# Delta rule: the fractal mixer's taps move from TensorE to ScalarE and VectorE, TensorE's rounds get a new order and more unread products

## The reference, cut to what matters

```
q, k, v = short_conv(x @ Wq), short_conv(x @ Wk), short_conv(x @ Wv)     # 4 taps along the sequence
...                                       # rotary, l2norm, chunks of 32: T = inverse of a triangular matrix
step:  u_t = ui - wi @ S;  o_i = qi @ S + attn @ u_t;  S_new = g * S + ki^T @ u_t      # 16 chunks, in sequence

def fractal_mixer(x, conv_w):
    out = 2.0 * x
    for i in range(4):
        dil = 2 ** i
        x_shift = jnp.pad(x, ((0, 0), (dil, 0), (0, 0)))[:, :l, :]
        out = out + x_shift * conv_w[i, :, 0] + x * conv_w[i, :, 1]
    return out
frac = rmsnorm(fractal_mixer(x, frac_conv_w), mixer_norm_w)
return core + sigmoid(x @ frac_gate_w + frac_gate_b) * frac
```

## Time and profile before

| what | us |
|---|---|
| median of three runs | 2610.29 (2605.36 to 2612.67) |
| the profiled execution | 2605.69 |
| its span | 2603.9 |
| first state step of round 2 to that of round 3 | 68.0 |
| rounds 3, 4, 5 | 71.0 each |
| rounds 6, 7, 8 | 74.4, 66.1, 56.0 |

### The profile page before, as it was taken

One profiled execution on the slowest core, in us unless ns is written; L12 is line 12 of the kernel. 1 busy time (PEld: TensorE's weight loads), 2 busy tenths in 40 slices (PEclk: granted clock), 3 DMA queues, 4 the chain that ended last, 5 costly groups with the idle time before them and its releaser, 6 DMA issues. The chain is left out here.

```text
span 2603.9 us, 56605 instructions
## 1 busy us (share of the span) xinstructions
PE 2413.8 (93%) x20854; PEld 2007.2 (77%) x20854; DVE 1696.0 (65%) x4060; ACT 1216.3 (47%) x3095; POOL 1334.0 (51%) x1465
## 2 busy tenths in 40 slices
PE   4899999999999999878999999988899999999998
PEld 3788888888888888756777877756677778778776
DVE  4576777767677767576767767326756746747664
ACT  2656666666666666455444445114333333332332
POOL 3676776767676767256555555214522323322322
PEclk8999999999999999989999999988999999999999
DMA  4000100000000000012112111206112112212211
GB/s 141 7 10 9 45 17 11 9 10 10 10 10 9 9 5 5 15 31 45 42 47 49 36 53 43 55 31 187 33 52 68 62 42 74 66 42 62 64 39 58
DMA packets 156688, 105.05 MB, mean 40 GB/s; under 512 B 85168, under 2 KB 134832, under 8 KB 156416
## 3 DMA queue, kind: packets, MB, share of 16 engines
q1 hardware_dynamic: 131072, 62.83, 8.9%
q10 hardware_dynamic: 25344, 38.60, 4.8%
HBM read 80.51 MB, written 20.88 MB: 39 GB/s over the span
## 5 line engine op out<-in xcount | busy, mean ns | idle before, releaser
L920 POOL TENSOR_TENSOR a_bm<-a_bias,a_mask_add 128x512 f32<-128x512 f32 (+3 forms) x512 | 437.8, 871 | 191.0 <-DVE a_nm L674 186.0
L1529 POOL TENSOR_TENSOR m_hid_part<-m_hid,m_hid_part 128x512 fp32r<-128x512 f32 x176 | 239.5, 1361 | 564.1 <-ACT m_hid_part L1438 561.0
L830 ACT ACTIVATE a_S<-a_S,a_nm 128x512 f32<-128x512 f32 (+3 forms) x512 | 289.2, 565 | 346.4 <-DVE a_nm L674 343.6
L674 DVE CUSTOM_DVE_ANT_0 a_S<-a_S,a_bm,a_nsn 128x512 f32<-128x512 f32 (+3 forms) x512 | 275.4, 545 | 141.2 <-PE a_S L438 136.9
L461 PE MATMUL a_O<-a_v,a_PT 128*128 128x64 f32 x2560 | 342.4, 265 | 0.0
L461 PEld LDWEIGHTS a_O<-a_v,a_PT 128*128 128x128 f32 x2560 | 328.4, 193 | 0.0
L1450 ACT ACTIVATE m_hid<-m_G 128x512 f32<-128x512 f32 x176 | 105.4, 599 | 408.4 <-PE m_G L1384 371.3
L438 PE MATMUL a_S<-a_kT,a_qT 128*128 128x384 f32 (+3 forms) x1024 | 284.3, 359 | 3.5 <-DVE a_nm L674 3.0
L1401 PE MATMUL m_Y<-m_hid_part,m_down_high 128*128 128x512 f32 x704 | 257.3, 406 | 11.9 <-POOL m_hid_part L1529 11.1
L1611 DVE TENSOR_TENSOR m_hid<-m_hid,m_U 128x512 f32<-128x512 f32 x176 | 121.0, 687 | 223.6 <-PE m_U L1384 189.7
L1384 PE MATMUL m_G<-m_in,m_gate_high 128*128 128x512 f32 x704 | 251.5, 398 | 1.6 <-POOL m_up_low L1523 1.6
(11 more groups left out here) (314 smaller groups left out, 5240.2 us busy)
## 6 DMA issues: line engine op xcount, KB each, us to landing
m_spread<-s_w ACTq DMA_DIRECT2D x64, 256.0 KB, 3.3
m_spread<-s_w ACTq DMA_DIRECT2D x128, 128.0 KB, 2.9
a_x<-in_x SPq DMA_DIRECT2D x32, 128.0 KB, 2.1
s_hT<-a_hT SPq DMA_DIRECT2D x32, 128.0 KB, 2.1
d_x<-in_x SPq DMA_DIRECT2D x8, 512.0 KB, 4.8
d_h<-s_hT SPq DMA_DIRECT2D x8, 512.0 KB, 5.4
s_xg<-d_xg SPq DMA_DIRECT2D x8, 512.0 KB, 3.1
d_x<-s_xg SPq DMA_DIRECT2D x8, 512.0 KB, 4.5
```

The costliest lines, as they stand in the source:

```text
L674: dve.tensor_tensor_reduce(S[:, n % S_SLOTS, 0:w], SB[n % 2][:, 0:w], bm[:, n % BM_SLOTS, 0:w], -1.0, nsn[:, tile % 2, h:h + 1], ALU.add, ...
L830: act.activation(S[:, n % S_SLOTS, 0:w], S[:, n % S_SLOTS, 0:w], ACT.Exp, scale=-1.0, bias=nm[:, tile % 2, h:h + 1], accum_out=den[:, tile ...
L920: pool.tensor_tensor(bm[:, n % BM_SLOTS, 0:w], bias[:, h, L - w:L], mask_add[b % 2][:, 0:w], ALU.add).then_inc(s["bm_ready"], 1)
L1529: pool.tensor_tensor(hid_part[1][:, q % H_SLOTS], hid[:, q % G_SLOTS], hid_part[0][:, q % H_SLOTS].bitcast(F32), ALU.subtract).then_inc(hi ...
```

## The change

The mixer's sum leaves PE. ACT makes the first tap of each half of the features from the input in SBUF into a new buffer `mx` (`tap`, two pieces for a batch, an activation of 128x512 each). DVE adds the four shifted taps (`mix`, two pieces of four `scalar_tensor_tensor` of 128x512, each behind the one before by a semaphore). PE's `mixer` becomes two transposes of `mx` and moves one round later, to lag F, with `frac`, `fve`, `frs` and `xg` behind it. The diagonal matrices and the ten instructions that made them go. SP's DMAs of `xg` out and of `x` in move one round later too, and its load of the next input waits for `mix_ready`, `proj_psum` and `gates_psum` in place of `mixer_psum`.

PE's table gets a new order: `proj` 4 goes from segment 0 to the end of segment 1, `au` 1 from segment 2 to segment 1, `core` 0 comes before `TZ`, `uw` before `qkT` in segments 8 to 10. Five `warm` pieces are added in segments 1, 4, 6, 8 and 10, of one unread product each, in every round that has a batch in the recurrence. `fast` becomes three products for batch 6 and stays one for batch 7. `warm` takes a bank of the ring as the others do. ACT's table follows.

```diff
-            ("step", 0, R), ("fast", 0, R), ("M", 1, R), ("qp", 0, R), ("proj", 4, IN), ("au", 0, R),
-            ("step", 1, R), ("fast", 1, R), ("M", 2, R), ("mixer", 0, IN), ("M", 3, R),
-            ("step", 2, R), ("fast", 2, R), ("M", 0, R), ("au", 1, R), ("z", 0, IN),
-            ("step", 3, R), ("fast", 3, R), ("proj", 5, IN), ("z", 1, IN), ("au", 2, R),
-            ("step", 4, R), ("fast", 4, R), ("qp", 1, R), ("z", 2, IN), ("Z", 0, F),
-            ("step", 5, R), ("fast", 5, R), ("hold", 0, K), ("hold", 1, K), ("hold", 2, K), ("hold", 3, K), ("onT", 0, K), ("onT", 1, K), ("z", 3, IN), ("mixer", 1, IN),
-            ("step", 6, R), ("fast", 6, R), ("TZ", 0, F), ("core", 0, K), ("au", 3, R),
+            ("step", 0, R), ("fast", 0, R), ("M", 1, R), ("qp", 0, R), ("au", 0, R),
+            ("step", 1, R), ("fast", 1, R), ("M", 2, R), ("warm", 0, R), ("au", 1, R), ("M", 3, R), ("proj", 4, IN),
+            ("step", 2, R), ("fast", 2, R), ("M", 0, R), ("z", 0, IN), ("mixer", 0, F),
+            ("step", 3, R), ("fast", 3, R), ("proj", 5, IN), ("z", 1, IN), ("au", 2, R), ("mixer", 1, F),
+            ("step", 4, R), ("fast", 4, R), ("qp", 1, R), ("Z", 0, F), ("warm", 1, R), ("z", 2, IN),
+            ("step", 5, R), ("fast", 5, R), ("hold", 0, K), ("hold", 1, K), ("hold", 2, K), ("hold", 3, K), ("onT", 0, K), ("onT", 1, K), ("z", 3, IN), ("mixer", 2, F),
+            ("step", 6, R), ("fast", 6, R), ("core", 0, K), ("TZ", 0, F), ("warm", 2, R), ("au", 3, R), ("mixer", 3, F),
             ("step", 7, R), ("fast", 7, R), ("qkT", 0, IN), ("uw", 0, F), ("attn", 0, F),
-            ("step", 8, R), ("fast", 8, R), ("mixer", 2, IN), ("qkT", 1, IN), ("uw", 1, F),
-            ("step", 9, R), ("fast", 9, R), ("core", 1, K), ("qkT", 2, IN), ("uw", 2, F),
-            ("step", 10, R), ("fast", 10, R), ("mixer", 3, IN), ("uw", 3, F), ("qkT", 3, IN),
+            ("step", 8, R), ("fast", 8, R), ("uw", 1, F), ("warm", 3, R), ("qkT", 1, IN),
+            ("step", 9, R), ("fast", 9, R), ("core", 1, K), ("uw", 2, F), ("qkT", 2, IN),
+            ("step", 10, R), ("fast", 10, R), ("uw", 3, F), ("warm", 4, R), ("qkT", 3, IN),
...
-                        unread(fill(name, i, b), B - b)
+                        unread(fill(name, i, b), 1 if b == B - 1 else 3)
...
+                        pe.wait_ge(mix_ready, KD * (b + 1))
                         o = fill(name, i, b)
                         for k in range(KD):
-                            at = PAD + i * P
-                            for j in range(5):
-                                back = 0 if j == 4 else 2 ** j
-                                last = pe.matmul(o[:, k * P:(k + 1) * P],
-                                                 h[b % 2][:, k, at - back:at - back + P], diag[:, k, j],
-                                                 start=j == 0, stop=j == 4)
+                            last = pe.transpose(o[:, k * P:(k + 1) * P], mx[:, k, i * P:(i + 1) * P], ident[:])
...
+                        act.activation(mx[:, i], h[b % 2][:, i, PAD:], ACT.Copy, scale=own[:, i:i + 1]).then_inc(mix_tap, 1)
...
+                        dve.wait_ge(mix_tap, KD * b + i + 1)
+                        for j in range(4):
+                            at = PAD - 2 ** j
+                            ins = dve.scalar_tensor_tensor(out=mx[:, i], in0=h[b % 2][:, i, at:at + L],
+                                                           scalar=frac[:, i, j, 0:1], in1=mx[:, i],
+                                                           op0=ALU.mult, op1=ALU.add)
...
-            ("S", 10, R), ("x1", 1, K),
-            ("S", 11, R), ("fve", 0, IN), ("attn", 1, F), ("low", 0, IN),
-            ("S", 12, R), ("attn", 2, F), ("low", 1, IN), ("attn", 3, F), ("xg", 0, IN),
+            ("S", 10, R), ("x1", 1, K), ("mix", 0, IN),
+            ("S", 11, R), ("fve", 0, F), ("attn", 1, F), ("low", 0, IN), ("mix", 1, IN),
+            ("S", 12, R), ("attn", 2, F), ("low", 1, IN), ("attn", 3, F), ("xg", 0, F),
```

More of the change, by code:

```diff
@@ L1842, in delta_phase @@
         ACT_ROUND = [
[L1843 to L1846, removed]
+            ("ocopy", 0, K), ("ocopy", 1, K), ("M", 1, R), ("silu", 0, IN), ("silu", 1, IN),
+            ("M", 2, R), ("osq", 0, K), ("silu", 2, IN), ("M", 3, R), ("proj", 4, IN),
+            ("M", 0, R), ("silu", 3, IN), ("z", 0, IN), ("frac", 0, F),
+            ("proj", 5, IN), ("z", 1, IN), ("frac", 1, F),
             ("z", 2, IN), ("silu", 4, IN), ("rsq", 0, IN),
-            ("onT", 0, K), ("onT", 1, K), ("z", 3, IN), ("rsq", 1, IN), ("frac", 1, IN),
-            ("rsq", 2, IN),
+            ("onT", 0, K), ("onT", 1, K), ("z", 3, IN), ("rsq", 1, IN), ("frac", 2, F),
+            ("rsq", 2, IN), ("frac", 3, F),
             ("qkT", 0, IN), ("uw", 0, F), ("rsq", 3, IN),
-            ("frac", 2, IN), ("qkT", 1, IN), ("uw", 1, F),
-            ("qkT", 2, IN), ("uw", 2, F), ("silu", 5, IN),
-            ("frac", 3, IN), ("uw", 3, F), ("qkT", 3, IN),
+            ("uw", 1, F), ("qkT", 1, IN), ("tap", 0, IN),
+            ("uw", 2, F), ("qkT", 2, IN), ("silu", 5, IN), ("tap", 1, IN),
+            ("uw", 3, F), ("qkT", 3, IN),
             ("proj", 0, NX), ("gm", 0, F),
@@ L1866, in delta_phase @@
             ("S", 9, R), ("qk", 3, IN), ("conv", 5, IN),
-            ("S", 10, R), ("x1", 1, K),
-            ("S", 11, R), ("fve", 0, IN), ("attn", 1, F), ("low", 0, IN),
-            ("S", 12, R), ("attn", 2, F), ("low", 1, IN), ("attn", 3, F), ("xg", 0, IN),
-            ("S", 13, R), ("vb", 0, IN), ("conv", 0, NX), ("xg", 1, IN),
-            ("S", 14, R), ("vb", 1, IN), ("conv", 1, NX), ("xg", 2, IN), ("gates", 0, NX), ("xg", 3, IN)]
+            ("S", 10, R), ("x1", 1, K), ("mix", 0, IN),
+            ("S", 11, R), ("fve", 0, F), ("attn", 1, F), ("low", 0, IN), ("mix", 1, IN),
+            ("S", 12, R), ("attn", 2, F), ("low", 1, IN), ("attn", 3, F), ("xg", 0, F),
+            ("S", 13, R), ("vb", 0, IN), ("conv", 0, NX), ("xg", 1, F),
+            ("S", 14, R), ("vb", 1, IN), ("conv", 1, NX), ("xg", 2, F), ("gates", 0, NX), ("xg", 3, F)]
         POOL_ROUND = [
             ("kb", 0, F), ("gxm", 0, F), ("ors", 0, K), ("nb", 0, IN), ("rot", 0, IN), ("rot", 1, IN), ("rrn", 0, IN),
-            ("rot", 2, IN), ("rrn", 1, IN), ("rot", 3, IN), ("rrn", 2, IN), ("rrn", 3, IN), ("frs", 0, IN),
+            ("rot", 2, IN), ("rrn", 1, IN), ("rot", 3, IN), ("rrn", 2, IN), ("rrn", 3, IN), ("frs", 0, F),
             ("off", 0, IN), ("inv", 0, IN), ("inv", 1, IN)]
         INV_STEPS = [range(1, 8), range(8, HALF - 1)]
-        RINGED = {"fast", "hold", "proj", "gates", "mixer", "z", "v", "qkT", "gram", "attn", "uw", "gm", "qp", "M", "onT", "core", "Z", "TZ"}
+        RINGED = {"warm", "fast", "hold", "proj", "gates", "mixer", "z", "v", "qkT", "gram", "attn", "uw", "gm", "qp", "M", "onT", "core", "Z", "TZ"}
         def drained(name, i, b):
-            return {"fast": None, "hold": None, "proj": (proj_ready, 6 * b + i + 1), "gates": (gates_read, b + 1),
+            return {"warm": None, "fast": None, "hold": None, "proj": (proj_ready, 6 * b + i + 1), "gates": (gates_read, b + 1),
                     "mixer": (frac_copied, TT * b + i + 1), "z": (zm_ready, TT * b + i + 1),
@@ L2273, in _ @@
                 link(dve.tensor_reduce(own[:], frac[:, :, :, 1], AX.X, ALU.add))
-                link(dve.tensor_scalar(own[:], own[:], 2.0, None, ALU.add))
-                for k in range(KD):
-                    for i in range(5):
-                        w = own[:, k:k + 1] if i == 4 else frac[:, k, i, 0:1]
-                        dve.tensor_scalar(diag[:, k, i], ident[:], w, None, ALU.mult)
+                dve.tensor_scalar(own[:], own[:], 2.0, None, ALU.add).then_inc(own_ready, 1)
                 dve.wait_ge(rot_ready, 1)
@@ L2296, in _ @@
                         ins.then_inc(conv_ready, 1)
+                    elif name == "mix":
+                        dve.wait_ge(mix_tap, KD * b + i + 1)
[4 more added lines that the diff above has]
+                                                           op0=ALU.mult, op1=ALU.add)
+                            if j < 3:
+                                link(ins)
+                        ins.then_inc(mix_ready, 1)
                     elif name == "gates":
```

30 lines of the change are left out of this document (21 added, 9 removed).

## The result

The changed kernel takes 2701.45 us (median of four runs, 2696.24 to 2702.68) against 2611.35 for the kernel before beside it (four runs): 1.0346 times, interval 1.0324 to 1.0368. It is slower, as forecast, but by 90 us where 18 were predicted, and the time lies outside the range of 2592 to 2646. The profiled execution took 2702.64.

A forecast was written before the change was run, and what follows sets the result against it. PE's own work was taken to bound a full round: 64.3 + 8.05 of waits = 72.3 us. Terms +3.4 - 4.8 + 6.0 + 9.6 + 4.8 + 1.6 = +20.6 on 2605.69 gave 2626.3, stated as 2628; range 2592 to 2646.

The forecast's parts named there:

- Bound and PE's own sum: Full round: PE's own work bounds it; without mixer products, with transposes and `warm`, 64.3 us, a gain of 6.7 before new waits.
- The four waits: PE in a full round: new waits at `au` 0 1.85, `z` 0 1.1 more, `z` 3 1.3, `uw` 0 3.8; sum 8.05 us.
- the price for steps: DVE's added `mix` work, 50.8 to 57.1 us a round, delays no PE step: no cost, states stay in time.
- a sign of being wrong: PE's steps waiting for DVE's `S` in the profile after, which would mean the `mix` pieces are not free.
- Rival 2: Before `uw` 0: DVE's `x1` 0 frees the bank in time, 19 us less than without clock falls, 2593; chance 0.22.
- The clock: Rounds 3 to 7: one 6.8 us stretch at 1.2 GHz each, from `uw` 0's wait, 3.2 us each; net +9.6.
- The upper bound of +26: Upper bound of the net clock cost over rounds 3 to 7, for two stretches at 1.2 GHz in a round.
- Rival 3: Two stretches at 1.2 GHz in each round, the second at `z` 0's wait: 5 x 3.2 more, 2644; chance 0.08.
- The ends: Rounds outside 3 to 7: rounds 0 and 1 +3.4, round 2 -4.8, round 8 +4.8, round 9 +1.6 us.

## Why the prediction was right or wrong

**Bound and PE's own sum: right.** A full round without low clock was forecast at 72.3; round 6 of the kernel with filled waits is 72.3. That it agrees to 0.1 is luck: `warm` costs 0.22 (1413.26 to 1413.48) and not the 0.32 I took, 0.5 less a round, and something else makes up for it.

**The four waits: right, three of them to 0.1 us.** `au` 0 1.81 (forecast 1.85), `z` 0 1.22 (1.25), `uw` 0 3.89 (3.9 derived, 3.8 taken). `z` 3 differs by round, against a forecast of 1.3: it is 0.22 in round 4 and 2.1 in all over rounds 2 to 5 (group of L2016 above), but 1.3 in round 6, and 1.3 in round 6 of the kernel with filled waits. In round 4 DVE's copy of `Z` ended 2.3 us after PE's step 5 had begun (1416.28 against 1414.01), where I had taken the 3.5 of before.

**DVE: right in size, but not free.** A tap takes 749 ns (787 taken), a round 55.6 to 56.2 us (57.1). In rounds 3 to 6 the steps hardly wait for the states, and the run with the order alone is as slow without any tap on DVE. I had put the price for steps at nothing, though, and named a wait for `S` as a sign of being wrong. One is there, 1.30 us before step 14 of round 7 against 0.39 before. I had looked at DVE's idle time in round 5, not in round 7, where PE has less to do between the steps. Rival 2, that `x1` comes in time, didn't happen; moving `x1` shows that it would have been worth 39.8 us, not the 19 that I gave it, since the clock comes with it.

**The clock: this step failed.** I wrote: "I expect a stretch of 6.8 us at 1.2 GHz in each of rounds 3 to 7". A full round has three, of 13.7, 6.8 and 10.2 us. Over rounds 3 to 7 that is 161 us at 1.2 GHz where I had forecast 34, and net of the 13.7 of before some 63 us of time (at 0.43 us for each, below) where I had 9.6. The price of a microsecond at the lower clock was about right: 3.2 for 6.8 is 0.47; measured, (85.4 - 72.3) / 30.7 = 0.43. Their number and length were not, and for one cause. I read from the earlier trace rows that 2.9 us of nothing call it and 2.7 don't, so only `uw` 0's wait qualified. But the very same group had the counter-example, a fall in round 6 without any wait, between `M` and `M`, and I gave it no weight. The trace of before has another, which I had left out of the rows: ahead of round 2 the clock fell within the second of two waits, of 1.04 and 2.42 us, with four transposes between them.

```profile
1140.75 1.12 PE L2031 MATMUL d_R<-s_ident,d_qk 128*128 128x128 f32 x4 [2.42 <-DVE d_qk L2340]
...
1139.40:1146.30 6.90, 5.55 (x26) 5.55 (x27) 4.12 (x7) 2.23 (x7) 2.01 (x1) 0.51 0.00 0
```

A wait of 1.8 us with narrow work on both sides was enough, as the runs with `proj` 4 back and with the waits filled show. The stretch went on over the narrow work behind it, which in segment 1 is a step, `M`, `warm`, `au`, `M`, and it ended only 3.4 us into the dense work that came next (`proj` 4, from 1393.44). The upper bound of +26 therefore was the bound of a model, not of the traces.

**Rival 3** named the place that failed, `z` 0's wait, and gave it 0.08 and 2644. It had one more stretch but not the one at `au` 0, and lengths of 6.8 only. The Trainium skill, "TensorE: Matmul & The Clock Gate", Part 4, says that transposes don't count as PE-busy in the way that products do, and I had taken from it that the stretch around `z` 0 would fall too. The low stretch from 1400.24 to 1407.07 is there. But with the mixer as products in that place (the run with the order alone) the round still has one of 3.4 us there and the 13.7 us one unchanged. So the mixer's transposes explain at most half of the one and none of the large one.

**The ends.** Rounds 0 and 1: +7.8 against +3.4, above the bound of 6. Of it 1.1 lies ahead of the delta phase, whose first product starts at 1100.64 against 1099.58, and 6.7 in it. Counted from that first product, the run with filled waits has +6.0 and the one with the taps alone +3.5, so about half comes with the new order. I didn't take it apart further. Round 2: +0.7 against -4.8; it has a low stretch of 10.2 us in all. Round 8: +14.4 against +4.8. This is the clock again, and a place that I had not looked at: the end of round 7, where no batch is left to project. Its low stretch goes on for 37.5 us (1714.27 to 1751.82) and begins in step 14's new wait for DVE's state. That wait isn't needed for it: the run with the order alone, whose wait there is the 0.39 of before, has a low stretch of 27.3 us from 1731.11 on. What both kernels have lost is the mixer in segments 8 and 10 of that round, two pieces of 2.50 us of products, and little that is dense is left from there on, by my reading of the order. How much the wait adds, these runs don't part: sixteen products there, with the third one after each step, filled the wait and thickened the work at once, and brought round 8 from 67.8 to 56.4. What follows round 8: +3.0 against +1.6; I didn't look at it.

**In sum.** Of the 76 us between forecast and result, rounds 3 to 7 make 55 (71.0 against 15.6), round 8 makes 10, round 2 5.5, rounds 0 and 1 4. Filling the three waits brings back 70 of the 90 us. So the waits alone would have set the direction of a full round, by little (72.3 against 71.0), and most of the size came from the clock.
